# Expert weights split during the attention and kept in DRAM, lower gelu halves on POOL, three scatters ahead of the gathers

## The chip, the core and the metric

The kernel runs on one core of a Trainium2 chip. The metric is the device time of one launch in microseconds, the median over runs; one execution was also taken by the hardware profiler, and its rows are what this document reads. Engines: PE (TensorE), ACT (ScalarE), DVE (VectorE), POOL (GpSimd) and SP, which issues most DMAs.

## What is computed

Two layers over X [2, 1024, 128], each followed by a residual and a layer norm:

```python
# differential attention, 8 heads of 128
attn = softmax(Q1 @ K1.T * s) - lam * softmax(Q2 @ K2.T * s)
O    = rms_norm(attn @ V) * rms_scale * (1 - LAMBDA_INIT)
x    = layernorm(X + O.reshape(B, N, -1) @ Wo.T)
# expert choice: 8 experts, each takes cap = 256 of the 1024 tokens of a sequence
probs = softmax(x @ gate_w)                      # over experts
top_p, top_idx = top_k(probs.T, cap)             # per expert
y   = (gelu(x[top_idx] @ w1[e]) @ w2[e]) * top_p
out = layernorm(x + scatter_add(y, top_idx))
```

The result is that of float32. The kernel gets it from fp32r matmuls by splitting each operand in a rounded upper part and a lower part (what rounding took away) and adding three products (upper x upper, upper x lower, lower x upper).

## The kernel before

**Attention (0 to about 790 us).** A software pipeline over 128 tiles G = 0 to 127 (2 sequences x 8 heads x 8 blocks of 128 queries). For each tile PE makes the scores of both softmaxes (`scores`), DVE the row maxima, ACT the exponentials, POOL the factor of the second softmax (`factor`: three column operations), ACT scales with it (`scale`), POOL adds both (`combine`, L640, [128,1024]), and three to eight tiles later PE transposes and multiplies with X. Work that isn't per tile is put in by hand at fixed values of G or of G % 8. SP moves the prepared matrices of a head (m, ww) to DRAM in the first sequence and back in the second; its program is one list in order.

Sequence 0's gate, its choice of tokens and its first gathers run inside the attention of sequence 1. What is left behind the attention, the tail, is: the last tiles' output and layer norm, the gate of sequence 1, its choice of tokens, the sixteen expert jobs of both sequences (job q: expert q % 8, sequence q // 8), and the second layer norm.

**Expert jobs.** A job has two halves, so there are half steps n = 0 to 31 (q = n // 2). `ffn(n)` stands in the programs of PE, ACT and DVE:

- PE: `rows_in(q+1)` transposes the gathered rows of the next job (it waits for their DMA), `up(n)` makes 128x512 of the hidden layer in PSUM (6 matmuls of 256 columns), `down(n-3)` the second product of an earlier half, `rows_out` the transposes back.
- ACT: `g_hi` (gelu, rounded, L881) and the full gelu (L883, written in place in PSUM). `y_scale` for sequence 0.
- DVE: the lower part of the gelu, full less rounded, [128,512] (L1367). It counts the semaphore `g_split`. PE's `up(n)` starts with `need(pe, g_split, n - 1)`: it waits until the lower part of half n - 2 is done, whoever makes it, and `down(n)` waits for that of half n.

The results of sequence 0 are added in DRAM by POOL's indirect DMAs (`scatter(q)`, two issues each, L668); those of sequence 1 by matmuls with one-hot matrices (`mix`, L1876). The rows of both are fetched by POOL's indirect DMAs (`gather_rows(q, k)`, L651, two for each job), for sequence 1 not before its indices exist (`indices`, DVE, L1332).

**The choice of tokens of sequence 1.** A search for the 256th largest probability in eight levels: DVE compares and counts (L1242), makes `hit` (L1245), PE adds up the votes with one small matmul (`votes`, L1651), DVE makes the step and the next candidate (L1258, L1262). Then come the ties (`limit`, `offset`, `tokens` on PE, L1656 to L1669), `counts` (L1678), two `signs` on ACT (L837) and the indices. `LAST = [1, 2, 3, 5, 6, 8, 9, 11]` says which half steps stand between the levels: on PE `votes(lv)` stands behind `ffn(LAST[lv])`, and on ACT both `signs` stand between `ffn(11)` and `ffn(12)`.

**Expert weights.** SP loads w1 and w2 of an expert in float32 to one of four buffers (`raws`); the upper part is a copy with rounding, the lower part a subtraction. ACT rounds experts 0 to 3 (L845), DVE subtracts for 0 and 1 (L1172), POOL does the rest (L679, L686) between 806 and 831 us, with two gathers behind every second expert. Then POOL scatters jobs 0 and 1, gathers for sequence 1, makes a row of token numbers (iota) and scatters jobs 2 to 7.

**POOL around the end of the attention.** `norm_end(t)` (L632, L634) makes four tiles' output factors, on which DVE's last sums (`add_out`, L1071) wait; between them stand gathers of sequence 0: numbers 2 to 6, then 7 and 8.

## Time and profile before

| | |
|---|---|
| median of 3 runs | 909.22 us (909.1 to 910.31) |
| the profiled execution | 909.54 us, span of the core 907.8 us |
| PE, ACT, DVE, POOL busy | 866.8, 748.7, 692.2, 639.6 us |
| mean granted PE clock | 0.986 of 2.4 GHz |
| DMA | 30.66 MB, mean 34 GB/s |

Times in the rows are microseconds from the start of the span. A line of a timeline is: start, busy time, engine, line of the kernel, operation, what it writes and reads, shapes, count, and in brackets how long the engine had been idle before it and what ended that. Lines merged under one start are consecutive instructions of one kind.

### The profile page before, as it was taken

What the parts mean: (1) busy time and instruction counts of PE and PEld (TensorE: products, weight loads), DVE (VectorE), ACT (ScalarE), POOL (GpSimd) and SP (SyncE); (2) the same over time, 40 slices, a digit from 0 to 9 for tenths busy, and PEclk for the clock granted to TensorE, in tenths of its full rate; (3) what the DMA queues carried; (4) which work ended last, traced back from release to release, by engine and by line L of the source; (5) the groups of instructions that cost most, each with busy time, mean ns of one, the idle gap of its engine ahead of it and who ended that gap; (6) DMA issues with size and microseconds to landing.
All of it is one profiled execution on the core that took longest, in us unless ns stands there. A gap on an engine that the chain in (4) does not pass through costs nothing.

```text
span 907.8 us, 14912 instructions
## 1 busy us (share of the span) xinstructions
PE 866.8 (95%) x4598; PEld 729.4 (80%) x4598; DVE 692.2 (76%) x1163; ACT 748.7 (82%) x1449; POOL 639.6 (70%) x1031
## 2 busy tenths in 40 slices
PE   6889999999999999999999999999999999877995
PEld 5668888888888888888888888888888888776984
DVE  5777777777777777777777768778898787578675
ACT  3888898888888888888889888988888889665754
POOL 1777767667776777676778866667776677769782
PEclk9999999999999999999999999999999999979898
DMA  6010010101010101001010020000000001332233
GB/s 180 13 43 16 30 31 1 59 1 58 1 59 1 47 13 36 12 19 30 1 30 1 19 58 18 15 18 16 7 24 1 19 1 44 114 82 48 50 37 99
DMA packets 41663, 30.66 MB, mean 34 GB/s; under 512 B 5825, under 2 KB 39649, under 8 KB 41585
## 3 DMA queue, kind: packets, MB, share of 16 engines
q1 hardware_dynamic: 38256, 26.44, 9.7%
q0 software_dynamic: 3328, 3.28, 2.5%
q8 instruction: 37, 0.61, 0.3%
q14 instruction: 42, 0.34, 0.1%
HBM read 20.14 MB, written 9.57 MB: 33 GB/s over the span
## 4 chain that ended last, share of the span: by engine, by line
PE 81%; POOL 6%; DVE 5%; issue 4%; ACT 2%; DMA 1%; POOLq 0%; SPq 0%; DVEq 0%; ACTq 0%
PE t_ps L1580 11%; PE ring_a L1541 6%; PE ring_a L1543 6%; PE ring_a L1542 6%; PE ring_b L1541 6%; PE ring_b L1543 6%; PE u_ps L1541 6%; PE ring_b L1542 6%; PE u_ps L1543 6%; PE u_ps L1542 6%; PE o_ps L1541 2%; PE o_ps L1542 2%; PE o_ps L1543 2%; PE x_ps L1541 2%; PE x_ps L1543 2%
## 5 line engine op out<-in xcount | busy, mean ns | idle before, releaser
L640 POOL TENSOR_TENSOR attn<-prob 128x1024 f32<-128x1024 f32 x128 | 307.4, 2402 | 173.5 <-ACT prob L799 161.8
L1056 DVE TENSOR_TENSOR at_lo<-t_ps,at_hi 128x512 fp32r<-128x512 f32 x253 | 174.1, 688 | 100.7 <-ACT at_hi L782 100.4
L1049 DVE TENSOR_REDUCE negmax<-ring_a 128x1 f32<-128x1024 f32 x128 | 156.7, 1224 | 58.6 <-PE ring_a L1543 55.7
L782 ACT ACTIVATE at_hi<-t_ps 128x512 fp32r<-128x512 f32 x253 | 151.6, 599 | 39.8 <-PE t_ps L1580 38.7
L1049 DVE TENSOR_REDUCE negmax<-ring_b 128x1 f32<-128x1024 f32 x128 | 156.2, 1220 | 2.7 <-PE ring_b L1543 1.1
L1580 PE MATMUL t_ps<-ident,attn 128*128 128x128 f32 x1012 | 152.1, 272 | 4.3 <-DVE at_lo L1056 4.1
L799 ACT ACTIVATE prob<-prob,coef 128x1024 f32<-128x1024 f32 x128 | 147.6, 1153 | 5.7 <-POOL coef L604 5.6
L1580 PEld LDWEIGHTS t_ps<-ident,attn 128*128 128x128 f32 x1012 | 124.4, 140 | 30.0 <-DVE at_lo L1056 9.4
L793 ACT ACTIVATE prob<-ring_a,negmax 128x1024 f32<-128x1024 f32 x128 | 143.1, 1118 | 4.6 <-DVE negmax L1049 4.1
L793 ACT ACTIVATE prob<-ring_b,negmax 128x1024 f32<-128x1024 f32 x128 | 142.4, 1112 | 0.6 <-DVE negmax L1049 0.5
L1541 PE MATMUL ring_b<-xt_hi,q_hi 128*128 128x512 f32 x256 | 112.0, 438 | 0.0
L1541 PE MATMUL ring_a<-xt_hi,q_hi 128*128 128x512 f32 x256 | 107.3, 419 | 0.5 <-ACT prob L793 0.4
L1543 PE MATMUL ring_a<-xt_hi,q_lo 128*128 128x512 f32 x256 | 101.3, 396 | 0.0
L1543 PE MATMUL ring_b<-xt_hi,q_lo 128*128 128x512 f32 x256 | 101.3, 396 | 0.0
L1542 PE MATMUL ring_a<-xt_lo,q_hi 128*128 128x512 f32 x256 | 100.5, 393 | 0.0
L1542 PE MATMUL ring_b<-xt_lo,q_hi 128*128 128x512 f32 x256 | 100.4, 392 | 0.0
L1541 PE MATMUL u_ps<-at_hi,xk_hi 128*128 128x512 f32 x248 | 97.8, 394 | 2.0 <-DVE u_lo L1062 2.0
L1543 PE MATMUL u_ps<-at_hi,xk_lo 128*128 128x512 f32 x248 | 97.3, 392 | 0.0
L1542 PE MATMUL u_ps<-at_lo,xk_hi 128*128 128x512 f32 x248 | 96.6, 390 | 0.0
L596 POOL TENSOR_TENSOR rs<-psum,neg_one 128x1 f32<-128x1 f32 x128 | 70.5, 551 | 14.7 <-ACT prob L793 14.5
L814 ACT ACTIVATE osq<-o_ps 128x256 f32<-128x256 f32 x117 | 44.9, 384 | 38.3 <-PE o_ps L1543 38.2
L624 POOL TENSOR_TENSOR fac<-var_o,neg_half 128x1 f32<-128x1 f32 x116 | 63.7, 549 | 16.5
(450 smaller groups left out, 1792.6 us busy)
## 6 DMA issues: line engine op xcount, KB each, us to landing
attn<-in_L_ffn_w SPq DMA_DIRECT2D x12, 256.0 KB, 3.3
ww_dram<-ww_hi SPq DMA_DIRECT2D x8, 192.0 KB, 2.5
ww_dram<-ww_lo SPq DMA_DIRECT2D x8, 192.0 KB, 2.9
ww_hi<-ww_dram SPq DMA_DIRECT2D x8, 192.0 KB, 2.4
ww_lo<-ww_dram SPq DMA_DIRECT2D x8, 192.0 KB, 2.5
wq_s<-in_L_attn_Wq SPq DMA_DIRECT2D x8, 128.0 KB, 2.7
wk_s<-in_L_attn_Wk SPq DMA_DIRECT2D x8, 128.0 KB, 3.1
xres<-in_L_attn_X SPq DMA_DIRECT2D x2, 512.0 KB, 6.3
```

Source lines behind the costliest of these rows:

```text
L596: pool.tensor_tensor(rs2[:, par:par + 1], psum2[:, par:par + 1], neg_one[:, :], ALU.pow).then_inc(rs2_ready, 1)
L624: pool.tensor_tensor(fac[:, par:par + 1], var_o[:, par:par + 1], neg_half[:, 0:1], ALU.pow).then_inc(fac_ready, 1)
L640: pool.tensor_tensor(attn[:, t % AB, :], prob[:, t % 2, 1, :], prob[:, t % 2, 0, :], ALU.add).then_inc(attn_ready, 1)
L782: act.activation(at_hi[:, g % 2, half * GT:(half + 1) * GT, c], t_bank(t, half)[:, :].rearrange("p (k q) -> p k q", q=P), ACT.Copy).then_i ...
L793: act.activation(prob[:, par, m, :], ring[m][:, :], ACT.Exp, bias=negmax[:, par, m:m + 1], accum_out=sums).then_inc(prob_ready, 1)
L799: act.activation(prob[:, par, 1, :], prob[:, par, 1, :], ACT.Copy, scale=coef[:, par:par + 1]).then_inc(scaled_ready, 1)
L1049: dve.tensor_reduce(negmax[:, par, m:m + 1], ring[m][:, :], axis=AX.X, op=ALU.max, negate=True).then_inc(negmax_ready, 1)
L1056: dve.tensor_tensor(at_lo[:, g % 2, k, c], t_bank(t, half)[:, :].rearrange("p (k q) -> p k q", q=P), at_hi[:, g % 2, k, c].bitcast(F32), A ...
L1541: pe.matmul(dst, a_hi, b_hi, start=start, stop=False)
L1542: pe.matmul(dst, a_hi, b_lo, start=False, stop=False)
L1543: return pe.matmul(dst, a_lo, b_hi, start=False, stop=stop)
L1580: last_t = pe.transpose(t_bank(t, half)[:, k * P:(k + 1) * P], attn[:, t % AB, kk * P:(kk + 1) * P], ident[:, :])
```

## The change

1. **Weights.** POOL does both parts of every expert's weights during the attention of tiles 8 to 71: a copy at G % 8 = 3 and 6, a subtraction at 4 and 7, always behind `combine`. SP loads one matrix (512 columns) at a time to one half of `raw_a`, and stores both parts to a DRAM tensor `w_parts` (`keep_parts`). Behind the last scores SP loads the parts of experts 0 to 3 to their places (`load_parts`), and those of 4 to 7 behind the stores and loads for sequence 1. The splits by ACT, DVE and POOL in the tail are gone.
2. **Lower parts of the gelu.** For halves 0 to 13 (`NP = 14`) ACT writes the full gelu to one of four SBUF buffers and POOL subtracts (`g_lower`); DVE does halves 14 to 31 as before. `g_split` is counted by whoever does it.
3. **Order on POOL.** Gathers of sequence 0: numbers 2 to 7, then 8 to 10, then 11 to 15 behind the row statistics; then the iota, then the fourteen lower parts with the scatters of jobs 0, 1 and 2 behind halves 6, 8 and 10, then the sixteen gathers of sequence 1, then scatters 3 to 7.
4. **PE.** 26 matmuls whose result nobody reads (`idle_work`) at five places between the attention and the search. Behind the last vote the order is `down(9)`, `limit`, `rows_in(7)`, `up(12)`, `offset`, `up(13)`, `tokens`, `counts`, `rows_out(4)`, `down(10)`, then from `ffn(14)` on.
5. **ACT.** The copy of the probability rows stands ahead of the load of the gelu table.

```diff
+            def keep_parts(e):
+                for w, v in enumerate((w1[e]..., w2[e]...)):
+                    c = 2 * e + w
+                    need(sp, w_kept, 32 * c)
+                    sp.dma_start(raw_w.rearrange("p (f c) -> p f c", f=FT), v).then_inc(w_raw_in, 16)
+                    sp.wait_ge(w_split, c + 1)
+                    for part, t in enumerate((raw_hi.bitcast(F32), raw_w)):
+                        sp.dma_start(w_parts[e, part][:, w * F:(w + 1) * F], t).then_inc(w_kept, 16)
+            def load_parts(e):
+                need(sp, w_in[e % WSEM], 32 * (e // WSEM))
+                for part, t in enumerate((w_hi[e], w_lo[e])):
+                    sp.dma_start(t..., w_parts[e, part]).then_inc(w_in[e % WSEM], 16)
...
+            sp.wait_ge(w_kept, 64 * E)
+            sp.wait_ge(scores_ready, 2 * TILES)
+            for e in range(E // 2):
+                load_parts(e)
+            store_x1(1); store_pn(1); store_rows(1); load_vals(1)
+            sp.wait_ge(u_ready, 31)
+            for e in range(E // 2, E):
+                load_parts(e)
...
+            def w_round(e, w):
+                pool.wait_ge(w_raw_in, 16 * (2 * e + w + 1))
+                need(pool, w_kept, 32 * (2 * e + w))
+                pool.tensor_copy(raw_hi, raw_w).then_inc(w_hi_done, 1)
+            def w_lower(e, w):
+                pool.tensor_tensor(raw_w.bitcast(F32R), raw_w, raw_hi.bitcast(F32), ALU.subtract).then_inc(w_split, 1)
+            def g_lower(n):
+                q, f = n // 2, slice(n % 2 * 2, n % 2 * 2 + 2)
+                pool.wait_ge(g_hi_done, n + 1)
+                pool.wait_ge(gelu_ready, n + 1)
+                pool.tensor_tensor(g_lo[q % 2][:, f, :], g_full[n % HOTS], g_hi[q % 2][:, f, :].bitcast(F32),
+                                   ALU.subtract).then_inc(g_split, 1)
...
-            for n in range(2, 7):
+            for n in range(2, 8):
                 gather_rows(n // CT, n % CT)
             norm_end(END)
-            for n in range(7, 9):
+            for n in range(8, 11):
                 gather_rows(n // CT, n % CT)
             norm_end(END + GT)
...
+            for n in range(11, CT * E):
+                gather_rows(n // CT, n % CT)
+            pool.wait_ge(t_ready, 250)
+            pool.iota(tok_row, ...).then_inc(row_ready, 1)
+            for n in range(NP):
+                g_lower(n)
+                if n in (6, 8, 10):
+                    scatter((n - 6) // 2)
             gather_ready(1)
...
-            for q in range(2, E):
+            for q in range(3, E):
                 scatter(q)
...
+            pe.wait_ge(y_added, 122)
+            idle_work(ring[0][:, 0:WWN], 4)
             x1_transposes(1, 0)
+            idle_work(ring[0][:, 0:WWN], 6)
             rows_in(0)
+            idle_work(ring[0][:, 0:WWN], 2)
             x1_transposes(1, 1)
...
+            idle_work(quarter[2][:, 0:WWN], 6)
             row_transposes(1, 0)
             row_transposes(1, 1)
+            idle_work(quarter[2][:, 0:WWN], 8)
...
             last = LAST[LEVELS - 1]
+            down(last - 2)
             limit(1)
+            rows_in((last + 1) // 2 + 1)
+            up(last + 1)
             offset(1)
+            up(last + 2)
             tokens(1)
             counts(1, 0)
             counts(1, 1)
-            for n in range(last + 1, 2 * JOBS + 2):
+            rows_out((last + 2) // 2 - 2)
+            down(last - 1)
+            for n in range(last + 3, 2 * JOBS + 2):
                 ffn(n)
```

## Rows read from the trace of the kernel before

**Rows 1.** The page, part 1: busy time and share of the span by engine.

```profile
PE 866.8 (95%) x4598; PEld 729.4 (80%) x4598; DVE 692.2 (76%) x1163; ACT 748.7 (82%) x1449; POOL 639.6 (70%) x1031
```

**Rows 2.** Busy time by stretch: PE, PEld, DVE, ACT, POOL, then clock, DMA share, GB/s.

```profile
400.00:700.00 300.00, 299.85 (x1566) 251.24 (x1566) 238.44 (x362) 262.92 (x493) 216.21 (x372) 1.00 0.07 19
```

**Rows 3.** The same for PE alone: length, busy time, granted clock, DMA share, GB/s.

```profile
796.00:800.00 4.00, 1.82 (x12) 1.00 0.18 53
800.00:807.00 7.00, 7.00 (x37) 0.53 0.05 12
...
838.00:844.00 6.00, 5.30 (x24) 0.50 0.39 37
...
850.00:893.00 43.00, 41.04 (x290) 1.00 0.39 64
```

**Rows 4.** Timeline in the attention, 157 to 160 us: POOL and the scaling behind it.

```profile
157.09 0.73 POOL L588 TENSOR_TENSOR ww_lo<-wvt_s,ww_hi 128x256 fp32r<-128x256 f32 x1
...
158.67 0.19 POOL L604 TENSOR_TENSOR coef<-coef,neglam 128x1 f32<-128x1 f32 x1
...
159.46 1.15 ACT L799 ACTIVATE prob<-prob,coef 128x1024 f32<-128x1024 f32 x1
```

**Rows 5.** Waits, 60 to 480 us: who for whom, total, times, longest.

```profile
ACT prob L799 <- POOL coef L604: 1.1, 4, 0.3
```

**Rows 6.** Timeline of POOL, 794 to 803 us: second end factor, last row statistics.

```profile
794.56 0.20 POOL L632 TENSOR_TENSOR var_e<-ssq_e,es 128x4 f32<-128x4 f32 x1 [0.89 <-ACT osq L814]
...
801.77 1.04 POOL L563 TENSOR_TENSOR stat<-stat,neg_half 128x4 f32<-128x4 f32 x1 [0.81 <-DVE stat L1114]
```

**Rows 7.** Durations by line on POOL, ns: minimum/median/maximum, first and last start.

```profile
L686 POOL TENSOR_TENSOR at_lo<-attn,at_hi x6: 1271/1281/1292, 819.1 to 830.1; 128x512 fp32r<-128x512 f32 x6
L679 POOL CAST at_hi<-attn x6: 600/604/624, 817.9 to 828.3; 128x512 fp32r<-128x512 f32 x6
L668 POOL DMA_INDIRECT acc_dram<-prob,idx x4: 1548/1594/1648, 834.2 to 840.0; - x4
```

**Rows 8.** Timeline of DVE from 808 us: the first levels of the search.

```profile
808.42 1.28 DVE L1242 TENSOR_SCALAR_CACHE_REDUCE attn<-prob,jtab 128x1024 f32<-128x1024 f32 x1 [0.39 <-ACT prob L833]
...
812.75 0.68 DVE L1367 TENSOR_TENSOR at_lo<-ring_a,at_hi 128x512 fp32r<-128x512 f32 x1
813.34 0.15 DVE L1258 TENSOR_SCALAR step<-x_ps 128x1 int32<-128x1 f32 x1
```

**Rows 9.** Timeline of PE: last output, last vote, token matmul, half step 16.

```profile
793.56 0.34 PE L1543 MATMUL ring_b<-ww_hi,xk_lo 128*128 128x384 f32 x1
...
833.63 0.18 PE L1651 MATMUL x_ps<-hit,grp_b 128*128 128x1 bf16 x1
...
838.32 0.22 PE L1669 MATMUL x_ps<-tok_rows,pick 128*128 128x8 bf16 x2 [1.43 <-DVE pick L1313]
...
851.05 0.39 PE L1541 MATMUL ring_a<-xk_hi,q_hi 128*128 128x256 f32 x1 [1.07 <-DVE xk_lo L1339]
```

**Rows 10.** Timeline of ACT, 820 us: the two gelus of one half.

```profile
820.14 0.60 ACT L881 ACTIVATE at_hi<-ring_a 128x512 fp32r<-128x512 f32 x1
820.63 0.59 ACT L883 ACTIVATE ring_a<-ring_a 128x512 f32<-128x512 f32 x1
```

**Rows 11.** Indices of sequence 1, first and last of its 16 gathers, their landing.

```profile
841.08 0.17 DVE L1332 SCALAR_TENSOR_TENSOR idx<-red,tok_c 128x8 int32<-128x8 f32 x1
842.15 1.10 POOL L651 DMA_INDIRECT prob<-xg_dram,idx  x1 [0.62 <-DVE idx L1332]
...
863.08 1.01 POOL L651 DMA_INDIRECT prob<-xg_dram,idx  x1 [0.30 <-issue]
...
prob<-xg_dram,idx POOLq DMA_INDIRECT x16, 2.6
```

**Rows 12.** Timeline of DVE at 892 us: the sums, then the last scaling.

```profile
892.78 0.29 DVE L1132 SCALAR_TENSOR_TENSOR xres<-xres,attn 128x128 f32<-128x128 f32 x1 [1.54 <-DMA attn<-acc_dram]
...
893.83 0.42 DVE L1354 TENSOR_TENSOR u_hi<-ring_b,prob 128x256 fp32r<-128x256 f32 x1
```

More of the change, by code:

```diff
@@ L1362, in ffn @@
                     last_y.then_inc(y_scaled, 1)
-                if q < JOBS:
+                if q < JOBS and n >= NP:
+                    if n == NP:
+                        dve.wait_ge(g_split, NP)
                     f = slice(2 * half, 2 * half + 2)
```

106 lines of the change are left out of this document (41 added, 65 removed).

## Prediction

> **What bounds the kernel now.** Three views, in this order. The page's first part gives PE 95% of the span [rows 1], but a mean hides the stages, so the second view is the busy time by stretches. In the attention stage PE is busy 299.85 of 300 us at full clock while POOL works 216 of 300 [rows 2]: there PE is the bound, and what POOL does more costs nothing unless it makes PE late. After 796 us lie all of its half clock (0.50, the 1.2 GHz level) and its long gaps [rows 3]. The third view is the timeline of each engine after 796 us, where the chain of waits changes engine all the time. I read it as three sections. (a) 808.42 to 838.32 us, the threshold search for sequence 1: eight levels, 3.15 us each (808.42 to the last vote at 833.63) [rows 8, 9], then the ties and the token matmul. (b) The slot indices at 841.08, which release POOL's sixteen gathers at 842.15 [rows 11]; PE's first up-projection of sequence 1 starts at 851.05 [rows 9]. (c) From 851 on PE is busy 41 of 43 us at full clock [rows 3], and the last expert's scaling on VectorE at 893.83 waits its turn behind the sums that wait for the reloaded accumulator (892.78) [rows 12]. So what moves the start of (c) moves the end; what only shortens POOL's queue behind it gains 1.1 us at most (893.83 less 892.78 [rows 12]) before PE's own chain is the bound.
>
> **What is removed.** Weight work leaves the tail: eight ScalarE copies of [128,512] (0.60 each, as in [rows 10]), four VectorE subtractions (0.68, as in [rows 8]), and on POOL eight copies (0.60) and twelve subtractions (1.28) [rows 7], 20 us. None of it is late work. PE is back to back until 796 us, and the first wait of the search on weights never shows: I cost the removal at nothing before 808 us and count POOL's 20 us as room that is used again below.
>
> **Work added in the attention.** Sixteen copies and sixteen subtractions, 16 x (0.60 + 1.28) = 30 us of POOL, each right behind the combine. There POOL goes straight on to the factor that ScalarE's scaling waits for. How much room that has [rows 4]: with 0.73 us of extra POOL work in the same place the coefficient ends at 158.86 and the scaling starts at 159.46, 0.60 later. So the room is 1.33 us: a copy fits, a subtraction just does. In the worst places ScalarE waited 1.1 us in four times within 420 us [rows 5], and PE stayed at full occupancy. Bounds: 0 (no wait reaches PE) and 1.5 us (8 subtractions that land on a step with 0.2 us less room); I take 0, since PE shows no wait where this already happens [rows 2]. SP's added waits on the parts stand in front of the loads of the prepared matrices; those are wanted a step of 5.9 us later, and a transfer lands in about 3 us. The reloads (8 MB in two halves, behind the last scores and behind the row loads) are each issued over 10 us before PE wants the first of them: hidden, and without that cover some 5 us.
>
> **From 782 to 808 us.** POOL issues six gathers ahead of the first end factor (five before) and three ahead of the second (two before). A gather is 1.32 us of POOL; in front of the second factor POOL idled 0.89 us [rows 6], and the extra gather in front of the first costs 0.45 there. The second factor comes 0.95 late, the last sums 1.2 late (transposes and the filler matmuls lie between), the row statistics end at 803.9 instead of 802.81 [rows 6]. PE gives back: it ran at half clock from 800 [rows 3], and the table load moves behind the row copy. The search starts at 808.1 instead of 808.42. The 26 filler matmuls are of the shape of the last outputs, 0.34 us each and less when they overlap [rows 9]; all but the first four stand where PE waits anyway.
>
> **The search (a).** VectorE loses 0.60 us a half, twelve times, and alone would do a level in about 2.5 us: 1.28 count, 0.8 hit and the way over PE, 0.4 step and candidate [rows 8]. But the lower half of a gelu now comes from POOL, 1.28 instead of 0.60, and PE's up(n) waits for the lower half of n-2 before it starts (need g_split n-1, unchanged). PE works in order, so the votes stand behind that up(n), and POOL has three scatters of 3.68 us between (two issues of 1.6, with 0.17 and 0.3 before them [rows 7]). POOL's own sequence, from rows: statistics 803.9, five gathers and the iota to 811.4; then one half per round of up (0.9), two gelus (1.1) [rows 10] and POOL (1.27): half 6 ends at 824.0. Scatter 0 to 827.7, halves 7 and 8 to 830.2, scatter 1 to 833.9, halves 9 and 10 to 836.4, scatter 2 to 840.1, half 11 to 841.4. Hence up(9) at 829.1 and vote 6 behind it, up(11) at 835.3, vote 7 at 836.1 (833.63 before). The change also puts up(13) ahead of the token matmul: it waits for half 11, starts at 841.5, and the token matmul follows at 842.3 to 843.1 (838.32 before): **+4.0 to +4.8**. The saving on VectorE is lost in PE's queue.
>
> **From the indices to PE (b).** idx 2.8 us behind the token matmul (841.08 less 838.32): 845. ScalarE does both signs and only then the gelus of halves 12 and 13, whose lower halves POOL must make ahead of the gathers: copies 0.5, gelus 1.1, POOL 1.27, and 1.6 for the second: the first gather starts 4.3 us behind idx, at about 849.5 (842.15 before, +7.3). PE's up(16) waits for two jobs' rows, the fourth gather: 849.5 + 3 x 1.32 + 2.6 to landing [rows 11] + 0.4 = 856.4 (851.05 before): **+5.3**.
>
> **PE's last part (c).** PE is nearly idle for 6 us ahead of it. Before, a gap at 834 to 838 was followed by 6 us at 0.50 [rows 3]; here that falls on full work: 5 us at half clock cost 2.5. Bounds 0 and 3.7. POOL has five scatters left instead of six and ends about where it did (849.5 + 21.0 + 19.4 = 889.9), so the accumulator is there before PE's chain is, and the 1.1 us that it cost is saved. Sum: 5.3 + 2.5 - 1.1 = +6.7; by a sum that takes every wait in turn +5.9 (the token matmul 0.8 earlier). I take +6.0. The profiled execution took 909.54 us (span 907.8, 1.7 around it) and lies 0.3 above the median of 909.22: 909.54 + 6.0 = 915.5, **915.3 us** against the median's level. With the ends of the parts: 3.0 + 0 + 0 to 5.3 + 3.7 + 1.5 less 1.1, that is 912 to 918.5.
>
> **One rule against the trace.** The granted clock fell to 0.50 from 800 on, behind 4 us in which PE ran twelve matmuls, nearly all of them transposes, and was busy for 1.82 us [rows 3]. The Trainium skill ("TensorE: Matmul & The Clock Gate", Part 4: PE-mode transpose) says that transposes don't count as PE work for the clock in the way other matmuls do. That rule would leave only the fillers to hold the clock from 797 to 801.5, with gaps between them; whether they do is the second rival.
>
> **Rivals.** (1) *The search runs at VectorE's pace.* If POOL keeps up, eight levels of 2.5 us end 5 us sooner, the indices come at 836, the gathers (still 4.3 behind) at 840.5, up(16) at 847: -4, and 905.5 us. For it: VectorE really loses 7.2 us between 808 and 834, and the clock is held. Against it: it needs half 7 by 826 us, with a scatter and a half in front of it that cost 5 us [rows 7]; even with no scatter POOL's halves alone bring the gathers to 843. This is the case on the other side; it decides at whether PE's ninth up-projection waits for POOL. (2) *The fillers don't hold the clock at 800 us.* PE at 0.50 until 817, as before: the search starts 1.4 later and the end is 2.5 later: 918. The same place is taken by the attention's 1.5 us. (3) *It cancels*: the gathers' delay is partly covered because PE has less left to do (halves 10 and 11 are done ahead), the clock stays up through the gap: +3 less 2, 910 us.
>
> **How the numbers follow.** Forecast (slower, 912 to 918.5) 0.60; rival 2 (917 to 920) 0.15; rival 3 (907.5 to 911) 0.07; rival 1 (903 to 907) 0.18. Faster by over 0.2% 0.18, within 0.2% 0.07 (0.2%, 1.8 us, is about what a measurement of this kernel can tell from no change), slower 0.75. The range of 8 in 10 runs from 907 to 919: the forecast, rival 3, most of rival 2. The forecast's own range is 912 to 918.5.
>
> **What would show it.** Right: PE's up-projections 9, 11 and 13 each idle 2 to 3 us for POOL's subtraction, votes 6 and 7 directly behind them; VectorE's step waits for votes; first gather of sequence 1 at 848 to 851; PE idle for DMA before about 856; clock 0.5 behind it. The attention ends at the same time as before. Wrong: levels of 2.5 us throughout, or the indices before 840, or PE waits in the attention. The prediction fails if a scatter takes POOL much less than 3.7 us between two subtractions, or if up(n) is not held by POOL.

## The result, and the profile after

The changed kernel takes **921.68 us** (median of four runs, 921.26 to 924.11), beside 909.56 us for the kernel before in the same comparison: ratio 1.0138, 95% interval 1.0119 to 1.0157. It is slower by 12.1 us where 6.0 were forecast. The profiled execution is the longest of the four, 924.11 us with a span of 922.4, so its trace shows 2.4 us more than the median. Of its lateness against the trace of the kernel before, 0.6 us stand ahead of the first tile.

The page of the changed kernel (busy time by engine), to be read beside [rows 1]:

```profile
span 922.4 us, 15016 instructions
PE 875.3 (95%) x4622; PEld 736.1 (80%) x4624; DVE 687.0 (74%) x1145; ACT 744.4 (81%) x1441; POOL 666.4 (72%) x1057
```

POOL is 27 us busier, PE 8.5, VectorE and ScalarE are 4 to 5 us less busy, and PE's share is the same 95%. The page doesn't find the loss. The next view does: the starts of POOL's combine of one tile, laid beside each other in both traces. For tile 66 it is 413.31 before and 415.67 after; for tile 126 it is 772.15 and 778.23. So 6.1 us of the 14.6 by which this trace comes to its last product later are there at tile 126, in the attention, where I had put nothing. The second row below is the start after less the start before:

| tile | 0 | 10 | 16 | 24 | 32 | 66 | 67 | 69 | 126 | 127 |
|---|---|---|---|---|---|---|---|---|---|---|
| us | 0.6 | 0.6 | 0.9 | 1.6 | 2.3 | 2.4 | 5.8 | 6.1 | 6.1 | 7.4 |

Three different losses are in it: 1.7 us in small steps up to tile 32, 3.4 us at once at tile 67 and 1.4 at tile 127. (The last is made up for before the search begins, see e9.) Timeline of POOL in the changed kernel at tile 67 (start, duration, and in brackets the idle time before it with what ended it):

```profile
415.67 2.40 POOL L663 TENSOR_TENSOR attn<-prob 128x1024 f32<-128x1024 f32 x1 [1.81 <-ACT prob L824]
...
422.14 0.61 POOL L699 CAST raw_a<-raw_a 128x512 fp32r<-128x512 f32 x1 [4.07 <-DMA raw_a<-in_L_ffn_w]
...
425.12 2.37 POOL L663 TENSOR_TENSOR attn<-prob 128x1024 f32<-128x1024 f32 x1
```

and SP's queue in the same stretch:

```profile
417.96 0.32 SPq L418 DMA_DIRECT2D ww_hi<-ww_dram  x1
418.32 0.43 SPq L418 DMA_DIRECT2D ww_lo<-ww_dram  x1
418.80 0.43 SPq L451 DMA_DIRECT2D raw_a<-in_L_ffn_w  x1
```

POOL stands for 4.07 us in front of its rounding, because the raw weights of expert 7 are not there. Their load is one instruction behind load_ww(8), and that one waits for TensorE's 56th output (o_ready), which comes at 418. The waits of 60 to 480 us show who pays; before, the first of these pairs stood there with 1.1 us in all [rows 5] and the second with 0.6:

```profile
ACT prob L824 <- POOL coef L627: 8.6, 15, 3.3
DVE xres L1090 <- POOL fac L647: 6.7, 9, 3.8
```

In the search the picture is what the prediction described, a little longer. Timeline of POOL (three rows), then of PE:

```profile
832.97 1.65 POOL L691 DMA_INDIRECT acc_dram<-prob,idx  x1 [0.17 <-issue]
834.92 1.54 POOL L691 DMA_INDIRECT acc_dram<-prob,idx  x1 [0.31 <-issue]
835.98 3.02 POOL L711 TENSOR_TENSOR at_lo<-attn,at_hi 128x512 fp32r<-128x512 f32 x2
```
```profile
819.96 0.55 PE L1552 MATMUL ring_a<-xk_hi,q_hi 128*128 128x256 f32 x1 [2.70 <-POOL at_lo L711]
...
837.82 0.39 PE L1552 MATMUL ring_a<-xk_hi,at_hi 128*128 128x256 f32 x1 [2.56 <-POOL at_lo L711]
...
843.93 0.39 PE L1552 MATMUL ring_a<-xk_hi,at_hi 128*128 128x256 f32 x1 [0.89 <-POOL at_lo L711]
...
844.75 0.18 PE L1662 MATMUL x_ps<-hit,grp_b 128*128 128x1 bf16 x1
...
850.04 0.58 PE L1552 MATMUL ring_a<-xk_hi,at_hi 128*128 128x256 f32 x1 [2.17 <-POOL at_lo L711]
...
851.49 0.26 PE L1680 MATMUL x_ps<-tok_rows,pick 128*128 128x8 bf16 x2
```

A scatter holds POOL, two halves wait behind it, PE's up-projections 9, 11 and 13 wait for POOL, and the vote and the token product stand behind them in PE's order. A fourth wait stands at the start: up(2) waits 2.70 us for POOL's first half, which POOL begins at 818.54, behind the gathers and the iota. The last vote (844.75) answers to 833.63 and the token product to 838.32 in [rows 9]. From the first step of the search to its last it is 27.8 us (817.22 to 845.05), before 23.2. Indices and gathers, which answer to [rows 11]:

```profile
854.16 0.17 DVE L1343 SCALAR_TENSOR_TENSOR idx<-red,tok_c 128x8 int32<-128x8 f32 x1
...
855.57 1.27 POOL L711 TENSOR_TENSOR at_lo<-attn,at_hi 128x512 fp32r<-128x512 f32 x1 [5.58 <-ACT attn L903]
857.06 1.28 POOL L711 TENSOR_TENSOR at_lo<-attn,at_hi 128x512 fp32r<-128x512 f32 x1 [0.21 <-ACT attn L903]
858.48 1.09 POOL L674 DMA_INDIRECT prob<-xg_dram,idx  x1
```

The first gather starts 4.32 us behind idx (before: 1.07).

### The profile page after: what moved, and what is told of

It is laid out like the page before. It is cut to its first block, busy times and chain, and to the rows that moved or that the text cites. A ratio compares the mean times of both kernels' runs of the same rounds, so it can differ in the third digit from the quotient of the medians.

```text
span 922.4 us, 15016 instructions
## 1 busy us (share of the span) xinstructions
PE 875.3 (95%) x4622; PEld 736.1 (80%) x4624; DVE 687.0 (74%) x1145; ACT 744.4 (81%) x1441; POOL 666.4 (72%) x1057
## 3 DMA queue, kind: packets, MB, share of 16 engines
q1 hardware_dynamic: 45168, 43.22, 14.6%
## 4 chain that ended last, share of the span: by engine, by line
PE 82%; POOL 5%; issue 4%; ACT 3%; DVE 3%; another core or an unknown queue 1%; DMA 1%; SPq 0%; POOLq 0%; DVEq 0%; ACTq 0%
PE t_ps L1591 11%; PE ring_a L1552 7%; PE ring_a L1554 7%; PE ring_a L1553 6%; PE ring_b L1552 6%; PE ring_b L1554 6%; PE ring_b L1553 6%; PE u_ps L1552 6%; PE u_ps L1554 6%; PE u_ps L1553 6%; PE o_ps L1552 2%; PE o_ps L1553 2%; PE o_ps L1554 2%; PE x_ps L1552 2%; PE x_ps L1554 1%
```

## The experiments

Each run is compared with the kernel before on the same chip. They ran on three chips: e1 to e4 on one (before: 910.7), e5 to e8 on a second (910.6), all the others on a third (920 to 921), of which more below. On which chip the result itself was taken isn't on record (before: 909.56). So kernels of different chips are compared by their distance to the kernel before beside them: 12.1 us for the changed kernel.

| run | what it is | us | ratio, 95% interval |
|---|---|---|---|
| e1 | changed, all of keep_parts(7) early | 922.06 | 1.0118 [1.0094, 1.0142] |
| e2 | changed, NP = 0, scatters in a block | 912.04 | 1.0026 [1.0011, 1.0042] |
| e3 | changed, up(n) freed of POOL | 920.10 | 1.0117 [1.0094, 1.0140] |
| e4 | changed, scatters behind the gathers | 926.21 | 1.0173 [1.0156, 1.0190] |
| e5 | changed, one load early | 919.80 | 1.0102 [1.0085, 1.0119] |
| e6 | before, with the fillers | 910.08 | 0.9995 [0.9985, 1.0005] |
| e7 | e2 and e5 together | 909.39 | 0.9988 [0.9975, 1.0001] |
| e8 | e7, split one tile earlier | 907.43 | 0.9970 [0.9959, 0.9982] |

**e2: does POOL's part in the search cost the time?**

```
-    NP = 14
+    NP = 0
...
-            for n in range(NP):
-                g_lower(n)
-                if n in (6, 8, 10):
-                    scatter((n - 6) // 2)
+            for q in range(3):
+                scatter(q)
```

> The changed kernel with the fourteen lower gelu halves given back to DVE; the three scatters stand in one block ahead of the gathers, all else as changed. Theory B (votes and indices are late because PE's up-projection waits for POOL): PE no longer waits for POOL, last vote 3 us sooner, first gather of sequence 1 directly behind the indices and 8 to 9 us sooner, end 6 to 10 us sooner: 912 to 916 us. Rival (DVE's relief is worth what POOL's slowness costs, the delay is the moved up-projections and the clock): within 2 us of 921.7, the search longer by DVE's 0.6 us a half.

912.04, 1.3 us over the kernel before instead of 12.1: 10.8 us are gone. The first step to the last step of the search takes 23.1 us again (815.89 to 838.98), the indices come 30.0 us behind the first step, where the changed kernel has 36.9 and the kernel before 30.3. (In e2 the first step itself waits behind a lower half that VectorE makes, and stands 3.4 us behind the search's first count, in the other two 2.1 and 2.3. Counted from the first count, the indices come at 33.3, 39.1 and 32.7.) The waits in the search, from 800 us on, first in the changed kernel, then in e2 (the step of the search for its vote):

```profile
DVE step L1269 <- PE x_ps L1662: 11.4, 7, 3.6
...
PE ring_a L1552 <- POOL at_lo L711: 8.3, 4, 2.7
```
```profile
DVE step L1267 <- PE x_ps L1660: 0.9, 2, 0.6
```

So POOL's lower halves with scatters between them cost all of the tail's loss and 3 us of what the rest of the change gains: behind idx, e2 is 3.0 us shorter than before (idx to the last product on PE 53.6 us, before 56.7).

**e3 and e4: is it the wait on POOL's subtraction, or the scatters between?**

```
-                need(pe, g_split, n - 1)
+                need(pe, gelu_ready if n - 2 < NP else g_split, n - 1)
```

> The changed kernel, but up(n) of PE waits for ACT's second gelu of half n-2, which is what frees its PSUM bank, and no longer for POOL's subtraction of it, where POOL makes the lower half. POOL does the same work in the same order. Theory B: waits of up(2), up(9), up(11), up(13) for POOL go (2.7, 2.6, 0.9, 2.2 us), last vote and indices 3 to 5 us sooner, the first gather still about 4 us behind the indices; end 4 to 6 us sooner: 916 to 918 us. Rival (the wait of up(n) only stands in front of that of down(n), which needs the same lower half): the gain is taken back by the next down, under 2 us, 920 or more.

The median of 920.10 is 9.4 us over the kernel before instead of 12.1. The 2.7 us are less than the 4 to 6 of the theory, and the bare number stands with the rival (920 or more). The profiled execution is the fastest of four that spread from 917.8 to 923.6. The search's steps take 22.1 us in it, 1.1 less than before: without up(n) waiting, the relief of VectorE shows. It is given back between the last step and idx, 11.9 us against 7.1. Two waits of PE in e3 show where:

```profile
839.80 0.39 PE L1552 MATMUL ring_b<-at_hi 128*128 128x256 f32 x1 [2.53 <-POOL at_lo L711]
...
846.49 0.21 PE L1680 MATMUL x_ps<-tok_rows,pick 128*128 128x8 bf16 x2 [2.17 <-DVE pick L1324]
```

The first is down(9), which needs POOL's half 9, as the rival said. The second is the token product, which waits for an operation of VectorE that POOL held up (last section).

```
             for n in range(NP):
                 g_lower(n)
-                if n in (6, 8, 10):
-                    scatter((n - 6) // 2)
...
-            for q in range(3, E):
+            for q in range(E):
```

> The changed kernel with scatters 0, 1 and 2 put behind the sixteen gathers; the fourteen subtractions stay on POOL. Theory B with the scatters as the larger part of POOL's delay: last vote 4 to 5 us sooner, indices 6 sooner, first gather 6 sooner, but eight scatters of 3.87 us now end the queue behind the gathers and the accumulator comes last: end within 2.5 us of the changed kernel, 919 to 924 us. Rival (the subtractions alone hold PE): last vote and indices within 1.5 us of the changed kernel's, and the end 5 us later or more.

With the scatters out of the way POOL keeps up: first to last step 23.6 us and idx 30.7 behind the first, 6.2 us less than in the changed kernel. But the end comes later, 15.5 us over the kernel before instead of 12.1 and 2 us above the range of the theory (926.21 where 919 to 924 were expected), since now POOL's chain bounds it. Timeline of POOL, its last scatter, and two of the waits from 845 us on in e4:

```profile
900.10 1.55 POOL L691 DMA_INDIRECT acc_dram<-attn,idx  x1 [0.30 <-issue]
```
```profile
PE t_ps L1886 <- DVE u_lo L1368: 11.3, 3, 10.2
...
DVE xres L1149 <- DMA attn<-acc_dram: 10.4, 1, 10.4
```

VectorE waits 10.4 us for the sums that the late scatters write, and PE for VectorE. So it is the scatters between the halves, and both their places are bad as long as POOL has the halves: between them they hold the search, behind them the end. In e2 all six issues stand in POOL's idle time during the search and cost nothing.

**e1 and e5: the load of expert 7.** e1 moves all of keep_parts(7), with its waits for POOL, ahead of load_ww(8):

```
-                if 2 <= k < E + 2:
+                if 2 <= k < E + 1:
                     keep_parts(k - 2)
                 if H <= k + 1 < STEPS:
                     load_m(k + 1)
+                if k == E:
+                    keep_parts(E - 1)
                 if k == 11:
```

> The changed kernel with one block moved in SP's list: keep_parts of the last expert stands ahead of load_ww(8) and no longer behind it. In the changed kernel load_ww(8) waits for PE's output of tile 55, which comes at tile 68, while POOL wants the last expert's first matrix at tile 67: POOL sat 4.1 us for that DMA and all tiles from 67 on are 3.4 to 3.7 us later. Theory A (one queued wait on SP costs the attention 3.7 us): 921.7 - 3.7 = 918.0 us, the 4.1 us wait gone, the rest of the trace the same but for the shift. Rival (POOL's added 30 us of work slow the attention as a whole, and the DMA wait stands in an idle time): no more than 0.5 us gained, 921.2 or more, the tiles before and behind 67 slower each by a little.

922.06, 11.3 us over the kernel before: hardly a gain, and the theory seemed to fall. The trace shows why. The step at tile 67 is gone (combine 2.28 us late, as at tile 66), and 3.7 us come at tile 73. Timeline of e1, SP's queue and then PE:

```profile
448.22 0.32 SPq L418 DMA_DIRECT2D ww_hi<-ww_dram  x1
448.58 0.43 SPq L418 DMA_DIRECT2D ww_lo<-ww_dram  x1
449.12 0.37 SPq L411 DMA_DIRECT2D m_hi<-m_dram  x1
```
```profile
452.53 0.51 PE L1554 MATMUL x_ps<-xt_hi,m_hi 128*128 128x512 f32 x1 [1.93 <-DMA m_lo<-m_dram]
```

SP stood in the waits of keep_parts(7) until 443. Behind it came store_ww(7), then load_ww(8), which waits for that store to land (448.22), and only then load_m(10) at 449.12, which PE wanted at 450.6. In e5, below, load_m(10) is issued at 443.62. The queue had only passed its lateness on. e5 moves the one load that is wanted and leaves the waits where they were (`keep_raw` is that load alone, taken out of `keep_parts`):

```
...
+                if k == E:
+                    keep_raw(2 * (E - 1))
                 if k >= H:
                     load_ww(k)
```

> Of the changed kernel only one transfer moves: the load of the first raw half of expert 7 goes ahead of the load of W_v W_o for step 8 on SyncE, and the waits for POOL's split of it stay behind that load. Theory A (SyncE is held at a wait for TensorE's tile while POOL wants this load; 4.1 us at tile 67, of which 3.4 to 3.8 us reach the combines): the wait of POOL's rounding on the DMA goes, no step of more than 1 us stands at tile 67 or at tile 73, and the time is 2.4 to 3.8 us below the changed kernel's 921.7, so 918 to 919.5, some 9 us above the kernel before. Rival (the loads' order only passes the wait from one place to another, as when all of expert 7's transfers moved and 3.7 us came at tile 73 instead): over 921, and a step of over 2 us somewhere in tiles 64 to 80.

919.80, and 9.2 us over the kernel before instead of 12.1. The load is issued at 401.83 instead of 418.80, the combine of tile 67 is 2.10 us late, that of tile 74 2.11: no step at all. Net, the order of that one transfer cost 2.3 to 3.7 us in the traces and 2.5 to 2.9 by the medians (12.1 less 9.2; e2's 1.3 to the -1.2 of e7, below). The traces of e2, e3, e4 and e13 win back 1.1 us by tile 70. The profiled execution of the changed kernel didn't: PE's granted clock was 0.51 from 425.8 to 429.2 in it, right behind PE's wait of 1.9 us, and there is no such fall in the other four.

**e7 and e8: do the causes add, and what are the small steps?** e7 is e2 and e5 together:

> Both cures at once: VectorE makes all lower halves, the three scatters stand in one block ahead of the gathers (as in the run that gave 912.04, 1.3 above the kernel before), and the first raw load of expert 7 stands ahead of the load for step 8. If the two losses are apart and add: that run less the 2.4 to 3.7 us that tile 67 costs, so 1 to 2.5 us below the kernel before. Rival (the search waits for something else that has the same lateness, so that the end does not move with the attention): within 0.5 us of that run, 1 us above the kernel before.

909.39, 1.2 us below the kernel before, at the lower edge of what was expected and at the edge of the interval. e8 then moves POOL's split one tile earlier, since the steps at tiles 24 and 32 stood where the subtraction (1.30) is followed one tile later by POOL's part for W_v W_o (0.74):

```
-                    if s in (3, 6):
-                        w_round(e, s // 6)
-                    if s in (4, 7):
-                        w_lower(e, s // 7)
+                    if s in (2, 5):
+                        w_round(e, s // 5)
+                    if s in (3, 6):
+                        w_lower(e, s // 6)
```

> As the run before it in this list, and POOL's split stands one tile earlier in each step (rounding at tiles 2 and 5 of 8, subtraction at tiles 3 and 6), so that the subtraction of 1.3 us no longer stands one tile ahead of POOL's 0.74 us for W_v W_o. Theory (the 1.7 us that the combines lose up to tile 32 are these two beside each other and the rounding beside the lower parts of k): 1 to 1.7 us less than with the old places, combines at tile 40 within 1 us of where tile 0 stands against the kernel before. Rival (each of POOL's 1.9 us per chunk costs wherever it stands, since factors come late): within 0.4 us.

907.43, 2.0 below e7 (whose executions spread from 907.2 to 911.5) and 3.2 below the kernel before. From tile 0 to tile 40 its combines lose 0.4 us against the kernel before, in e7 1.6. So POOL's 30 us of work in the attention cost 1.7 us where the change put them and 0.4 one tile earlier. On this chip e8 beats both kernels.

The neighbour that I named isn't the whole cause. The two stand beside each other at tiles 39 and 40, 47 and 48 and so on as well, and nothing is lost there. What only the steps at tiles 23 and 31 have is VectorE's lower part of x (`xt_lo`) at the same time. Timeline of the kernel before, then of the changed kernel:

```profile
151.56 0.68 DVE L1042 TENSOR_TENSOR xt_lo<-xg,xt_hi 128x512 fp32r<-128x512 f32 x1
151.69 0.60 POOL L599 TENSOR_TENSOR coef<-rs,psum 128x1 f32<-128x1 f32 x1
...
152.36 0.19 POOL L604 TENSOR_TENSOR coef<-coef,neglam 128x1 f32<-128x1 f32 x1
...
153.43 1.17 ACT L799 ACTIVATE prob<-prob,coef 128x1024 f32<-128x1024 f32 x1
```
```profile
152.48 1.35 DVE L1061 TENSOR_TENSOR xt_lo<-xg,xt_hi 128x512 fp32r<-128x512 f32 x1
...
153.24 1.00 POOL L619 TENSOR_TENSOR rs<-psum,neg_one 128x1 f32<-128x1 f32 x1
...
154.81 1.15 ACT L824 ACTIVATE prob<-prob,coef 128x1024 f32<-128x1024 f32 x1 [0.33 <-POOL coef L627]
```

Beside VectorE's operation a column operation of POOL takes 0.60 us instead of 0.19, so already in the kernel before the coefficient ended at 152.55 and the scaling began at 153.43. The room was 0.88 us there and not 1.33, and a subtraction of 1.30 doesn't fit. The combine comes 0.44 us later at tile 23, and 0.25 more at tile 24, where the part for W_v W_o follows. The same is repeated at tiles 31 and 32. e8 moves the subtraction away from both neighbours, so no run tells what each is worth alone.

**e6: the fillers alone**, in the kernel before:

> The kernel before with only the change's 26 filler products on TensorE (4, 6, 2, 6 and 8 at the same places of its order, with the same wait for 122 additions). Theory (the fillers hold the granted clock of the stretch from 793 to 808 us, where the search waits for vectors and not for TensorE): the search starts within 0.3 us of 808.4, and the whole moves by 0 to -1.5 us, through faster products of the first halves. Rival (the fillers stand in front of transposes that others wait for, 26 products of about 0.1 us): +0.5 to +2 us.

910.08, no difference that can be told. The search's first step stands at 810.55 (810.74 before), with an attention that ran 0.5 later, so the section is 0.7 shorter. It is gone again at the indices, which come 33.5 us behind the first count (32.7 before). PE by stretch in e6 (length, busy time, clock, DMA share, GB/s), beside [rows 3]:

```profile
800.00:807.00 7.00, 6.67 (x53) 1.00 0.05 10
...
838.00:844.00 6.00, 4.22 (x20) 0.50 0.38 36
```

They hold the clock in 800 to 807 (0.53 before), and it is lost again at 838.

**A third chip.** The next ten runs fell on a chip on which the kernel before takes 920 to 921 us, 10 more. To see where, the kernel before was run there with a trace:

> The kernel before, unchanged, for a trace on the chip of this call. On a chip where the engines stand still behind the gathers: 919 to 921, a trace equal to the one shown up to idx at 841.1, and pauses of together some 10 us in waits that the profile puts down to nothing, between 845 and 880 us. On a chip without them: 909 to 911 and no such pause over 2 us.

921.58, 1.0012 [0.9993, 1.0032]. Up to idx (841.58, against 841.08 in [rows 11]) this is the same execution. Then PE's last product starts 68.2 us behind idx, where it was 56.7. The cured kernel e8 has 53.7 on the second chip; on this one it was run again:

> The kernel with all three cures (VectorE makes the lower halves, scatters in one block, first load of expert 7 early, POOL's split one tile earlier), unchanged from the run that gave 907.43. Where TensorE, ScalarE and VectorE don't stand still behind the gathers: 907.4, 3.2 us below the kernel before and 14 below the changed one. Where they do: the difference to the changed kernel stays 11 to 15 us, and the time against the kernel before is what these pauses make it (the last four runs, built on this one, were 3 to 8 us over the kernel before).

925.5, 1.0050 [1.0031, 1.0069], with 71.0 us from idx to PE's last product. PE in 860 to 870 us, in e8 and in the same kernel here:

```profile
860.00:870.00 10.00, 9.13 (x63) 8.14 (x62) 8.14 (x17) 4.58 (x11) 8.17 (x7) 1.00 0.27 41
```
```profile
860.00:870.00 10.00, 0.19 (x1) 0.53 0.27 42
```
```profile
869.81 0.69 PE L1883 MATMUL ring_b<-ident,osq 128*128 128x128 f32 x2 [10.40 <-issue]
```

(The first row has all engines, the second PE alone.) PE stood for 10.4 us in a wait that the profile puts down to nothing, ScalarE for 8.7 in the same time in one whose releaser it doesn't know; POOL and the transfers went on. All kernels on this chip have such pauses in 850 to 880 us, behind the first gathers: the kernel before 11.5 us of lengthening, the cured one 17.3. What causes them is open: they fall while POOL issues indirect transfers and where both kernels are the same code, but no experiment separated these. The Trainium skill ("Runtime: NRT & Kernel Launch", Instruction fetch mechanics) says that each engine's sequencer fetches its instructions in blocks through a DMA queue of its own; such a fetch that comes late would look like this, but no row here shows one that was waited for.

The changed kernel was run there again, and with the forecast for a chip with pauses:

> The changed kernel itself once more, as the mark for the three runs beside it, on whatever chip they get. In the last four runs all engines stood still for 10 to 16 us in all, behind the first gathers of the end, in waits that the profile puts down to nothing, and the kernel before took 920 instead of 910.6 there. If this chip has no such pauses: 921 to 922.5, 11 to 12 us over the kernel before, as measured first. If it has them: 930 to 940, again over the kernel before.

937.65, 1.0190 [1.0159, 1.0221]. Its trace has the same step at tile 67 (combines 1.75 us late at tile 66, 5.24 at tile 67, 4.2 from tile 72) and the same waits in the search (first step to idx 35.5 us, 1.4 less than in the first trace; see the search in the next section). The cures are worth 12.1 us here (937.65 less 925.5), and 15.3 by the comparisons with the kernel before on the other chips (12.1 over it, 3.2 under it). But the gain over the kernel before does not hold: 3.2 us faster on the second chip, 4.2 slower on this one.

The other seven runs there are of four kernels, each with one thing changed in that of e8. Their times carry the pauses; what stands ahead of idx can be read.

> The kernel of the run with POOL's split one tile earlier (907.43, 3.2 below the kernel before), and the load of the first four experts' parts waits for the last transposes of the attention instead of the last scores, some 10 us later. In all kernels with this load TensorE's granted clock fell to 0.6 to 0.8 for some 4 us at tile 127 and its combine came 1.0 to 1.4 us late; the kernel before, with the same pause of 1.5 us ahead of the same products, did not show it. Theory A (the fall goes with the transfer of 4 MB at 360 GB/s beside the pause): the fall and the 1.2 us go, 906.0 to 906.8. Rival (the fall has another cause, or the load then comes late for the first half or lies on the gathers and norm of the end): within 0.4 us of 907.4, or over it.

e9 puts sp.wait_ge(t_ready, 256) ahead of the first reload. 925.0, 1.0050, the same as e14 without it. It was to show whether the fall of the clock at tile 127 comes from the reload (363 GB/s beside it in the changed kernel). PE in the changed kernel, and in e9 (all engines):

```profile
776.00:780.00 4.00, 2.46 (x13) 1.00 0.81 282
780.00:784.00 4.00, 3.41 (x11) 0.60 0.97 363
```
```profile
770.00:774.00 4.00, 2.29 (x12) 1.52 (x10) 1.63 (x3) 2.14 (x4) 3.35 (x7) 1.00 0.09 22
774.00:778.00 4.00, 3.58 (x12) 2.94 (x13) 1.06 (x2) 1.72 (x6) 2.83 (x7) 0.61 0.08 17
```

The clock falls without the reload beside it (17 GB/s), and in e10 and e12, with the reload, it doesn't (1.00 at this place). So the reload is not the cause. By the distance of the combines of tiles 126 and 127 (6.4 us without the fall, 7.1 to 7.9 with it) it is there in ten of twenty traces, and it comes and goes for one and the same code: it is there in the profiled execution of the changed kernel and in e8, and not in e13 and e14, their repetitions. The gap of PE ahead of it is 1.47 us with and without. What decides was not found. It doesn't make the execution longer: from tile 126 to the first count of the search it is 36.5 to 36.9 us in the ten traces with the fall and 36.6 to 36.7 in the seven others of kernels with this reload. Those seven have the clock at 0.50 for some 3 us later, beginning between 802.7 and 807.2, and take 1.1 us longer from tile 127 to the search. The earlier fall stands in the place of the later one. The three traces of the old attention (before, e6, e17) don't have it at tile 127, so something else of the change may have to do with it.

> TensorE's order behind the search as in the kernel before, again, beside the kernel that it is built on, on one chip. Expected as before: 0.5 to 1.5 us above it; rival: within 0.4 us. In the last four runs it was 3.6 to 5.5 us above the other three, so the part that is due to the order, and not to where the pauses fall, should show here.

e16 undoes the new order of PE behind the search. 928.87, 1.0086, 3.4 us over e14 on the same chip (its first run, e10, gave 928.62 beside 925.00 of e9). The indices come 0.6 us later behind the first step (31.1 against 30.5), the rest lies behind idx, with the pauses in it. The order is worth something, more than the 0.5 to 1.5 that I expected of it, in a size that the pauses blur.

> The kernel that gave 907.43 with the scatter of job 2 behind the gathers again, as before the change, so two and not three stand ahead. POOL's chain behind the gathers then has one scatter of 3.7 us more. Theory (POOL's last scatters do not bound the end while three stand ahead, and with two they do): 1.5 to 3.7 us later, 909 to 911. Rival (there is slack behind the gathers): within 0.5 us of 907.4.

e11, with the scatter of job 2 behind the gathers again, gives 925.02, like e14: no cost that shows under the pauses, and the theory of 1.5 to 3.7 us isn't confirmed.

> The kernel with POOL making six lower halves again, beside the one it is built on. In the last trace its search was 22.5 us from the first step to the last against 23.3, idx came 29.3 us behind the first step against 30.1, and the end could not be read. Expected 0.5 to 1.1 us below the run just before it in this list; rival (idx earlier by 0.8 us, but behind it TensorE bounds the end): within 0.3 us.

e15 lets POOL make six lower halves in its idle time ahead of the first scatter (NP = 6, with the freed wait of e3). 923.12, 2.4 below e14, where 0.5 to 1.1 were expected. First to last step 22.5 us and idx 29.3 behind the first step, against 23.6 and 30.5. Counted from the first count of the search, which doesn't stand behind a lower half of VectorE, idx comes at 31.5 against 33.9: all 2.4 us lie ahead of idx, and from there to PE's last product both take 71.0. That is the part of the idea that pays. Part of it may be the clock, which is at 0.50 for some 3 us in that stretch in the three traces with six halves and for some 7 in e14. Its first run was e12 (923.10), its third, with five rounds, e18:

> The kernel with all cures and POOL making six lower halves, which was 2.4 us below the one with none on the chip with pauses (923.12 and 925.5) and 1.9 above the kernel before. On a chip without pauses: 905.5 to 907, 3.5 to 5 us below the kernel before. On the chip with them: 921.5 to 924, 1 to 3 us above it.

923.03, 1.0046 [1.0030, 1.0063]. The three runs are 1.9 to 3.1 us over the kernel before on this chip. It was never timed on another one, so whether it beats e8's 907.43 there is open.

## Why the prediction was wrong in size

**What is removed at nothing, the reloads hidden**: right. No kernel shows a wait for the parts, and once the losses are cured (e8) the kernel is faster than the one before, on the one chip without pauses where that was timed.

**Attention at nothing**: wrong, and the largest miss. It has two terms. The first was POOL's room of 1.33 us for a subtraction of 1.28: I measured it at tile 24 and took it for all. At tiles 23 and 31 it is 0.88, because VectorE's `xt_lo` holds POOL up there (see e8), and what is late is carried into the next tile, where POOL's part for W_v W_o stands. The coefficient came 0.33 late there, and 1.24 once in the first step (tile 12), which cost 0.3. Cost 1.7 us in all, just over the upper bound of 1.5 that I had given and not used. The second is the failed step proper: "SP's added waits on the parts stand in front of the loads of the prepared matrices; those are wanted a step of 5.9 us later". I looked at what stands behind the new transfers and not at what they themselves stand behind. For the first seven experts nothing ahead of keep_parts waits as long; ahead of keep_parts(7) stands load_ww(8), which waits until 418, and POOL wants the raw weights at 418.1. 3.4 us at tile 67, 2.5 to 2.9 of them in the time.

**From 782 to 808 us**: 0.3 less was forecast, and the runs can't tell. The search's first count starts at 815.10, 6.7 later than in [rows 8], of which 6.1 were there at tile 126: the section is 0.6 longer. In the second pair of traces (e13 and e17) it is 0.7 shorter, and the kernel before alone differs by 1.0 between its two traces. The clock, 0.60 at 780 to 784 us, I didn't foresee; it is no effect of the reload and costs nothing by the first count (e9).

**The search (a)**: right in mechanism, in the profiled execution too small in size. Forecast of the vote 7: 836.1, or 28.0 behind the start of the search; measured 29.65 (815.10 to 844.75). Token product 34.2 to 35.0 behind it forecast, 36.4 measured. A scatter with its two halves takes 6.0 us on POOL (832.97 to 839.00), the sum was 6.2, so the places with scatters came out as forecast. The difference is there before the first of them: POOL's half 6 ends 17.7 us behind the start (832.8), forecast 15.9. Two things of that stretch I had not put in. One is the wait of up(2) for half 0, 2.70 us: e3, without it, makes its second step 4.5 us behind the start instead of 6.6. The other is half clock. PE by stretch in the changed kernel:

```profile
820.00:824.00 4.00, 4.00 (x19) 0.50 0.71 251
...
850.00:856.00 6.00, 4.11 (x18) 0.50 0.00 0
```

In 820 to 824 PE works full time at 0.50, behind a stretch (814 to 820) in which it was busy for 2.42 of 6 us and waited for POOL. The repetition e13 is the same code with the clock at 0.50 for some 3 us there (817.4 to 820.8) and not for some 7. Its half 6 ends 16.3 us behind the start, its last vote comes at 28.2 and its token product at 34.9, as forecast; e1 and e5, with some 7 us, have 17.6 and 17.9, 29.5 and 29.9, 36.3 and 36.6. Of the 1.4 us that half 6 gains, 0.6 are there when POOL begins its halves (2.9 behind the start instead of 3.4); the rest, 0.8, goes with the clock. So the last vote was put too early by 1.5 to 1.9 us in three of the four traces of this search, and by 0.2 in the fourth. e2, e3 and e4 show each link: without POOL's halves 23.1 us, without the wait 22.1, without the scatters 23.6.

**From the indices (b)**: first gather 4.3 us behind idx, measured 4.32. Token product to idx was 2.8 forecast, 2.67 measured; first gather to up(16) 6.9 and 6.83.

**PE's last part (c)**: forecast 2.5 for half clock less 1.1, measured 0.3 from up(16) to PE's last product (865.31 to 912.33, before 851.05 to 897.75). The half clock stood mostly ahead of up(16), from 849.1 to 859.3, where PE waits for rows anyway:

```profile
865.11 0.44 PE L1843 MATMUL o_ps<-ident,prob 128*128 128x128 f32 x2 [2.18 <-DMA prob<-xg_dram,idx]
865.31 0.36 PE L1552 MATMUL ring_a<-xk_hi,q_hi 128*128 128x256 f32 x1
```

The sum of the tail was forecast at +6.0. By the starts of PE's last product (+14.6, less 6.1 at tile 126) it is +8.5 in this trace: 0.6 up to the first count, 7.6 from there to up(16), where 5.7 were forecast, and 0.3. The accumulator's 1.1 us were saved as forecast: the sums start at 906.82, right behind the scaling. (Five scatters at 3.68 us are 18.4 and not the 19.4 of my sum; nothing hangs on it.)

**The rule on transposes**: the row behind it was right, what I made of it decided nothing. In the changed kernel the clock is 1.00 in 807 to 814, as in 800 to 807 of e6, with the fillers between the transposes; in [rows 3] it was 0.53. The second rival, that they don't hold it, is out in this execution and in e6; in seven others with the fillers, e13 among them, the clock was at 0.50 for some 3 us, beginning between 802.7 and 807.2 (before: some 7 us from 800.4, and in e17 some 17 from 799). The rule of the Trainium skill ("TensorE: Matmul & The Clock Gate", Part 4: PE-mode transpose) agrees with the traces, which don't prove it: nearly transposes alone lost the clock, transposes with fillers kept it in some, but the fillers also made PE busier (in e6 3.70 of 4 us in 796 to 800, before 1.82), and no run separates the two. The time gained was within the measurement (e6: 0.9995).

**The rivals.** (1) VectorE's pace of 2.5 us a level wasn't reached even by e3 (22.1 us for seven levels, 3.2 each): VectorE's own work isn't the whole of a level. It fell for the reason that I gave, but its price was wrong too: freed of all waits for POOL it gains 1.1 us, not 5. (2) Decided nothing: where the clock did fall, its search didn't start later (e9). (3) Out. In sum, by the median: forecast 6.0, measured 12.1. The attention gave 1.7 and 2.5 to 2.9; the 7.5 to 7.9 that are left are the tail, of which 6.0 were forecast (8.5 in the profiled execution, the slowest of the four).

## What to carry to other kernels

When transfers are added to a queue that an engine feeds in program order, look at both sides of each: who waits behind it, and what wait it stands behind itself in every step of the loop; and move the one transfer that is wanted, not the group with its waits (e1 against e5). Work for a half-idle engine is only free where it ends before that engine's next due time in every tile, and the room for it has to be read at every tile: here it was 1.33 us at one and 0.88 at its neighbour. Moved by one tile, 30 us of it cost 0.4 instead of 1.7. And before an engine off the path gets a link of the chain, list what else stands in its order: POOL's 1.3 us instead of VectorE's 0.7 was harmless and even gained (six halves, 2.4 us), with a 3.7 us scatter between every two of them it cost 10.4 us (e5 to e7) to 10.8 (the result to e2). Measure a section from an event that the change doesn't move: from the first step the six halves seem to gain 1.2 us, from the first count 2.4.

## What was not expected of the hardware

VectorE is held while POOL subtracts. Timeline of the changed kernel, two cumulative sums of the search, the second of which takes 2.68 us instead of 0.29, and POOL beside it:

```profile
846.01 0.29 DVE L1293 TENSOR_TENSOR_SCAN prob<-prob 128x64 f32<-128x64 f32 x1
...
847.46 2.68 DVE L1310 TENSOR_TENSOR_SCAN prob<-prob 128x64 f32<-128x64 f32 x1
```
```profile
848.17 1.82 POOL L711 TENSOR_TENSOR at_lo<-attn,at_hi 128x512 fp32r<-128x512 f32 x1
```

The scan ends at 850.14, POOL's subtraction at 849.99. e1, e5 and e13 have the same (2.68 to 2.70 us). In e3 it is the other scan (838.36, 2.78 us, to 841.14; POOL's subtractions end at 840.99) and an addition on 64 columns (843.40, 2.52 us instead of 0.25, to 845.92; POOL ends at 845.86). The scan of 847.46 begins 0.7 us ahead of POOL's subtraction in the record, beside the issue of a scatter; the scan at 846.01 stands beside such an issue too and takes 0.29, so an issue alone doesn't hold it. In the changed kernel the hold costs nothing: up(13) waits for the same subtraction (850.04) and the token product follows behind it without a gap (851.49). In e3 the first hold is covered by down(9), and the second costs 2.2 us (PE's wait for `pick`). In the attention the two slow each other: `xt_lo` on VectorE takes 1.35 us beside POOL's subtraction instead of 0.68 (see e8). The Trainium skill ("GPSIMD Engine Reference", 1. Specifications) says that the two engines share their way into SBUF and compete when VectorE reads two inputs from it or works in a mode with two ports; for the scans and `xt_lo`, which read two inputs, the traces agree, and show that a small instruction can wait until POOL's large one ends and not only be slowed. The addition reads one tensor and a column, and no run shows in which mode. In the kernel before POOL's subtractions were over at 831 us [rows 7], ahead of the scans (834.89 and 836.48), and both scans took 0.29.

The second thing is the chip: the same code of the kernel before took 909 to 912.5 us on two chips and 916.7 to 924 on a third. In the traces all but 0.5 us of the difference of 12 lies behind the indices. A gain of 3 us that is measured on one chip isn't one until it is seen on another.
